# Graph layer on one core: x is loaded behind chunk 0's node numbers on SyncE's queue, edge weights and targets on ScalarE's, and TensorE sorts chunk 0 from turn 8

## The reference

```python
edge_in = concat([h[row], h[col], dist], axis=1)      # 64 + 64 + 1 values per edge
e = silu(edge_in @ eW1 + eb1)                          # 128
e = silu(e @ eW2 + eb2)                                # 128
agg = segment_sum(e, row, num_segments=3125)
out = silu(concat([h, agg], axis=1) @ nW1 + nb1) @ nW2 + nb2
x = layernorm(x + out)                                 # called with h = x, row = src, col = dst, dist = edge_weight1
```

## Time and profile before

| what | us |
|---|---|
| time, median of three runs | 631.85 |
| the three runs | 632.32, 631.36, 631.85 |
| span of the profiled execution | 629.0 |
| the median less that span | 2.85 |
| PE, DVE, ACT, POOL busy | 530.9, 463.5, 355.5, 429.0 |

### The profile page before, as it was taken

The page is one execution under the profiler, slowest core; times in us unless marked ns, Lnnn a source line. Parts: engine busy times, 40 slices in busy tenths (PEclk is TensorE's granted clock), DMA queues, the critical chain, the costliest instruction groups (busy, mean ns, idle before and its releaser), DMA issues.

```text
span 629.0 us, 15166 instructions
## 1 busy us (share of the span) xinstructions
PE 530.9 (84%) x4653; PEld 447.6 (71%) x4653; DVE 463.5 (74%) x1364; ACT 355.5 (57%) x812; POOL 429.0 (68%) x465
## 2 busy tenths in 40 slices
PE   4942869879879989998998899889997888879795
PEld 3421658768768869887887778778776777769684
DVE  6987999988999899989888869797642533223356
ACT  5842555455555556755655555565556666656464
POOL 2337576566777777777777777777777777777750
PEclk9986899779999999999999999999999999999997
DMA  5211111111111121111121111111111121111111
GB/s 121 77 51 51 43 52 48 36 50 48 56 52 52 52 56 56 52 56 49 54 56 52 51 55 56 53 52 55 54 54 55 52 56 54 53 55 53 55 39 51
DMA packets 17215, 34.17 MB, mean 54 GB/s; under 512 B 8133, under 2 KB 9352, under 8 KB 17142
## 3 DMA queue, kind: packets, MB, share of 16 engines
q0 software_dynamic: 14080, 28.86, 16.0%
q1 hardware_dynamic: 2594, 3.40, 2.1%
q10 hardware_dynamic: 468, 0.96, 0.6%
HBM read 30.73 MB, written 2.40 MB: 53 GB/s over the span
## 4 chain that ended last, share of the span: by engine, by line
POOL 32%; DVE 25%; PE 21%; issue 16%; DMA 3%; DVEq 1%; SPq 0%; POOLq 0%
POOL q_rows L736 32%; PE layer_ps L749 9%; PE sort_ps L749 6%; PE seg_ps L749 5%; DVE load_hot L1212 3%; DVE agg L1283 3%; DVE count L1058 2%; DMA q_rows<-q_table,q_index 2%; DVE hot L1268 2%; DVE col_hot L1206 1%; DVE row_hot L1207 1%; DVE place L1102 1%; PE turn_ps L841 1%; DMA src_i<-in_src_dram 1%; DVE slot L1108 1%
## 5 line engine op out<-in xcount | busy, mean ns | idle before, releaser
L736 POOL DMA_INDIRECT q_rows<-q_table,q_index x440 | 419.4, 953 | 159.5 <-issue 127.6
L583 ACT ACTIVATE e<-layer_ps 128x512 f32<-128x512 f32 x110 | 65.7, 597 | 212.7 <-PE seg_ps L749 204.3
L1283 DVE TENSOR_TENSOR agg<-agg,seg_ps 128x125 f32 x416 | 93.3, 281 | 93.5 <-PE seg_ps L749 90.3
L749 PE MATMUL layer_ps<-hotT,p_table 128*128 128x128 bf16 x1320 | 158.8, 225 | 0.2
L749 PE MATMUL layer_ps<-ident_f,q_rows 128*128 128x128 f32 x440 | 126.7, 288 | 33.6 <-DMA q_rows<-q_table,q_index 32.8
L749 PE MATMUL seg_ps<-hot,e 128*128 128x125 f32 x880 | 125.1, 286 | 23.9 <-DVE agg L1283 23.9
L749 PEld LDWEIGHTS layer_ps<-hotT,p_table 128*128 x1320 | 122.3, 98 | 22.7 <-issue 2.3
L749 PEld LDWEIGHTS seg_ps<-hot,e 128*128 128x128 f32 x880 | 109.5, 196 | 27.3 <-issue 25.3
L749 PE MATMUL layer_ps<-w_sb,h 128*128 128x128 f32 x880 | 119.5, 279 | 0.0
L749 PEld LDWEIGHTS layer_ps<-w_sb,h 128*128 128x128 f32 x880 | 111.2, 193 | 4.6 <-issue 0.2
L749 PEld LDWEIGHTS layer_ps<-ident_f,q_rows 128*128 128x128 f32 x440 | 63.0, 143 | 44.3 <-DMA q_rows<-q_table,q_index 43.3
(11 more groups left out here) (193 smaller groups left out, 439.9 us busy)
## 6 DMA issues: line engine op xcount, KB each, us to landing
q_rows<-q_table,q_index POOLq DMA_INDIRECT x440
q_table<-q_in_sb SPq DMA_DIRECT2D x1, 784.0 KB
x_sb<-in_x_dram ACTq DMA_DIRECT2D x1, 700.0 KB
q_table<-q_in_sb SPq DMA_DIRECT2D x1, 616.0 KB
out_dram<-x_sb SPq DMA_DIRECT2D x2, 224.0 KB
out_dram<-x_sb SPq DMA_DIRECT2D x1, 252.0 KB
w_in<-in_edge_weight_dram SPq DMA_DIRECT2D x1, 185.9 KB
dst_i<-in_dst_dram SPq DMA_DIRECT2D x1, 185.9 KB
```

Of the source, the lines that this page charges most:

```text
L583: A.activation(e2[:, m % 2, :], e_of(m)[:], ACT.Silu).then_inc(e2_ready, 1)
L736: P.indirect_dma_start(q_rows[:, g % RING, j, :], None, q_table, bass.IndirectOffsetOnAxis(ap=q_index[:, GT * g + j:GT * g + j + 1], axis= ...
L749: return nc.tensor.matmul(o, lhsT, rhs, start=start, stop=stop, **kw)
L1283: D.tensor_tensor(o, o, seg_ps[:, j * LO:(j + 1) * LO], ALU.add).then_inc(agg_added, 1)
```

## The change

x goes to SyncE's queue, between chunk 0's node numbers and the other node numbers. Edge weights and targets go to ScalarE's queue, in the place where x stood, ahead of eW1. `WC_SLOT` becomes 8: the splits of the weight row are in turns 8 to 10 in place of 10 to 12, and the batches 0 to 6 of chunk 0's sort in turns 8 to 14, with two batches behind turn 14 in place of four.

```diff
-WC_SLOT = PQ_SLOTS - SPLITS - 2
+WC_SLOT = PQ_SLOTS - SPLITS - 4
...
             load_nodes(*CODED[0], src_in)
             for a, b in ROWS:
-                sp.dma_start(w_in[a:b, :], edge_weight.rearrange("(p t) o -> p (t o)", p=EP)[a:b, :]).then_inc(w_landed, 16)
-            for a, b in ROWS:
-                sp.dma_start(dst_i[a:b, :], dst.rearrange("(p t) -> p t", p=EP)[a:b, :]).then_inc(dst_in, 16)
+                sp.dma_start(x_sb[a:b, :], x.rearrange("(p b) f -> p (b f)", b=WIN)[a:b, :]).then_inc(x_in, 16)
             load_nodes(COL0[1], ECOL, src_rest_in)
...
             for a, b in ROWS:
-                act.dma_start(x_sb[a:b, :], x.rearrange("(p b) f -> p (b f)", b=WIN)[a:b, :]).then_inc(x_in, 16)
+                act.dma_start(w_in[a:b, :], edge_weight.rearrange("(p t) o -> p (t o)", p=EP)[a:b, :]).then_inc(w_landed, 16)
+            for a, b in ROWS:
+                act.dma_start(dst_i[a:b, :], dst.rearrange("(p t) -> p t", p=EP)[a:b, :]).then_inc(dst_in, 16)
```

## The result

| | before | after |
|---|---|---|
| time, median of 18 runs each, us | 631.30 | 632.57 |
| lowest and highest, us | 629.11, 632.34 | 630.96, 634.19 |
| ratio after to before, 95% interval | | 1.0023 [1.0012, 1.0034] |
| span of the profiled execution, us | 629.0 | 629.1 |

The changed kernel is slower by 0.23%, 1.45 us on 631.3 (0.8 to 2.1 us by the interval); the two medians alone differ by 1.27 us. The profiled execution of after took 630.96 us, the fastest of its 18 runs, so its span of 629.1 must not be set beside 629.0 as if the two stood for their kernels.

The account below looks back on a forecast made before the run. The start, VectorE's chain to the index, was taken to set the first gather and so the end. x's later landing put `summed` 0.62 us later; added to the runs' median of 631.85 this gave 632.5 us, range 630.7 to 633.9.

Parts of the forecast that it names:

- First gather sets the end, one for one: Whole run: a shift of GpSimd's first gather, at 39.27 us before, reappears in full at the end.
- last sign of being wrong: At the end: first gather shifts as said while the end moves by more than a microsecond otherwise, felling one for one.
- Node numbers earlier: VectorE's start: src_i no longer behind x, gain 1.55 us (5.5 in place of 7.03), bounds nothing to 2.5 us.
- x later: Landing of x on SyncE's queue: 8.6 us in place of 7.46, bounds 7.0 and 9.3.
- Where the two meet: VectorE's `summed` waits for TensorE's OFFSET behind x: 13.74 in place of 13.12, 0.62 us later; wait about 2.2 us.
- TensorE's pace: TensorE's first pairs: faster pace gives 0.5 us less, slow pace one pair longer 0.5 us more; neither taken.
- Sort at turn 8: TensorE stands 1.7 us at batch 0's sort; the end of the sort moves with VectorE alone, +0.62 us.
- Covers: Slack before the first gather: last product to 32.8, ScalarE's copy 34.0, store lands 38.7; cover shrinks 3.9 to 0.3 us, holds.
- second rival: Store of q_table becomes GpSimd's wait, first gather at 41.2, +1.9 us, 633.8 us; chance 0.27.
- first rival: x's load at the queue's best rate lands by 6.2, VectorE's own chain decides: -1.55, 630.3 us; chance 0.13.
- The third: At VectorE's start: weights hold up src_i as x did; costs nothing, lies within the forecast.

Follow-up runs that it names:

- experiment 4: Changed kernel with TensorE's OFFSET of chunk 0 placed ahead of its wait for x; 630.73 us, ratio to before 0.9988.
- experiment 1: Changed kernel with the sort beginning at turn 10 as before, so only the loads are moved; 632.42 us, ratio to before 1.0019.
- experiment 6: Changed kernel with 18 products of ones by ones on TensorE ahead of its wait for x; 630.47 us, ratio to before 0.9988.
- experiment 2: Kernel before with only the sort's first turn moved to 8, loads as before; 630.87 us, ratio to before 1.0001.
- experiment 7: Kernel before; src_i's second piece ahead of x on ScalarE's queue, OFFSET behind transposes, sort from turn 9, 14 products of ones before x's wait; 629.07 us, ratio 0.9959.

## Why the prediction was right or wrong

The time (632.5 forecast, 632.57 measured) fits better than the step behind it deserves. The median of before over 18 runs is 631.30 and not the 631.85 of the first three; the shift was 1.45 us where I had 0.62. A base 0.55 us too high and a shift 0.65 us too small (by the medians) nearly cancel, and that is luck. "No change" was given 0.60 and "slower" 0.27, and the measured 0.23% lies just on the slower side of the 0.2% at which I parted the two, with an interval across it.

- *First gather sets the end, one for one:* right, by the table above. Single executions stray around it: the profiled one of after had its first gather 1.75 us late and its last instruction 0.1 us late, so it made up 1.65 us on the way. Taken by itself this pair of profiles meets the last sign of being wrong that the prediction gave, an end that moves by more than a microsecond otherwise than the gather; the rule is held up by the runs of eight kernels, not by single spans. In the stretch from 60 to 110 us the execution of after has 37 gathers and that of before 36. Why it caught up was not tested.
- *Node numbers earlier:* right in sign and too small. I took 1.55 us by the weights' piece in x's place; it was 2.47 us, the upper bound, set by VectorE's constants. It changed nothing, as argued: the wait at `summed` is just longer, 4.02 us where I had about 2.2.
- *x later:* the mis-sized term. I had 8.6 with 7.0 to 9.3 as bounds; it was 9.69, outside. I counted weights, targets and eW1, and from them 0.16 to 0.29 MB more than before ahead of x; it was 0.54 MB (1.55 less 1.01), which at the 237 GB/s of the earlier trace rows is 2.28 us, and x let TensorE go 2.23 us later. What the sum left out is the 0.21 MB of other node numbers and small weights, which follow x on its own queue and ran beside its last rows; and it took 0.265 MB as already gone before, where it was 0.19 (1.01 less 0.825). On the engines' side it is as the Trainium skill has it ("DMA: Bandwidth & Descriptors", "Issuing engines are not separate DMA queues"): the two queues share what is there, and the trace agrees, 236 and 233 GB/s for either order. A fair sum would have counted the loads behind x too.
- *Where the two meet:* right, step by step. x to `summed` was 5.19 us where I summed 5.14, and experiment 4 shows that nothing but OFFSET ties VectorE to x up to there. Behind it experiment 4 brings out a second tie: with OFFSET ahead, TensorE's transposes begin at 10.77 and its turns later still, ScalarE's copies with them, and VectorE's way to the gather is 1.65 us longer, nearly all of it in the two waits shown there.
- *TensorE's pace:* priced at 0.5 us either way. As scatter between executions that was about right (pair 0 took 1.41 to 1.92 us in experiment 1, before and after). As a cost it was far too small: experiment 6 takes 2.26 us out of the way from x to `summed`, as all 13 transposes run slow too, which I had taken as given.
- *Sort at turn 8:* right. 1.57 us of standing where I had 1.7, and worth nothing that could be measured (experiment 2).
- *Covers:* right. Last pair's product 33.85 for 32.8, store 35.05 for 34.0, both later by the microsecond that x was later. The second rival, the store as the wait, did not happen: GpSimd was released by `q_index` in all kernels, and its first gather starts 1.08 to 1.09 us behind `q_index` in each. The first rival, x at the best rate, was refuted by the landing itself. The third, that src_i would still be held up, fell with 4.56.

So the cause is settled as the forecast had it, with one term, x's landing, too small by 1.1 us.

## What to carry to other kernels

A load moved ahead of another helps only if the engine that waits for it is not tied, a few steps on, to the load that was pushed back: follow both chains to the instruction where they meet, and ask whether that small instruction (here two products of 0.4 us) can stand ahead of the other's wait. When two orders of the same loads are compared, sum all the bytes in flight until the load in question is whole, also those behind it on its own queue. And where TensorE starts slowly and waits for data, as here, products with no use ahead of that wait can shorten the way behind it.

## What the runs showed of the hardware that was not expected

- 12 transposes of 125x128 took 2.76 us as TensorE's first work and 1.50 us behind 18 products (experiment 6), and behind 14 products also 1.50 us (experiment 7); pair 0 took 1.92 and 1.10 us. The factors, 1.84 and 1.75, lie near the two between TensorE's levels of 1.2 and 2.4 GHz. The column of the granted clock reads 1.00 from 9.69 to 14.70 us in the changed kernel and from 9.69 to 12.60 us in experiment 6, so it does not show the slow level. But the traces' own list of clock levels, which the column counts as 1.00 where it has no entry, begins at 14.52 us in the changed kernel and at 7.99 us in experiment 6, both times with the full level, and the pace changes there: between pair 0 (1.92 us) and pair 1 (1.10 us) in the one, amid the products of ones (two matmuls each in the trace) in the other, of whose matmuls 15 fall in 3 us and then 9 in 1 us. That the slow pace is the clock's rests on list and durations agreeing. The view by stretch of these matmuls in experiment 6:

```profile
2.00:5.00 3.00, 3.00 (x15) 1.00 0.92 278
8.00:9.00 1.00, 1.00 (x9) 1.00 1.09 154
```

  In experiment 7 the list begins at 4.87 us, though its products begin at 1.84 us as in experiment 6, so how many products are enough cannot be read from one execution. The Trainium skill ("TensorE: Matmul & The Clock Gate", "Part 1: The HAM clock gate") calls the slow level the default that activity releases; experiments 6 and 7 agree.
- With the same order of loads and no change on the DMA side, x let TensorE go at 7.46 in the profile of before and at 6.79 in that of experiment 2: such a landing is known to no better than some 0.7 us from one profile. In the changed kernel and experiments 1, 4 and 6, which load alike, x's last row ended at 8.36, 8.41, 7.96 and 8.40.
